# Routing 28 of 32 tiles of the last mixture of experts during the attention before it

## What is computed

```
x = x + tanh(g_xattn[1]) * _L1_xattn_ref(_layernorm(x), ctx_768, ...)   # 16 heads of 8, 1601 keys
x = x + tanh(g_ffn[1])   * _L1_ffn_ref(_layernorm(x), ...)              # below

gate_scores = x @ Wg + bg                      # 8 experts
top1   = argmax(gate_scores, axis=-1)
h = relu(einsum('btd,edh->beth', x, W1) + b1)  # 128 -> 512, of the chosen expert
y = einsum('beth,ehd->betd', h, W2) + b2       # 512 -> 128
out = einsum('betd,bte->btd', y, onehot(top1))
```

## Time and profile before

| | |
|---|---|
| median of 3 runs | 2914.64 us (2913.44 to 2914.93) |
| profiled execution: own time | 2913.21 us |
| profiled execution: span | 2911.2 us |
| its mean granted TensorE clock | 0.901 |
| PE / DVE / ACT / POOL busy | 83% / 75% / 72% / 43% of the span |

### The profile page before, as it was taken

One profiled execution on the slowest core, in us unless ns is written; L12 is line 12 of the kernel. 1 busy time (PEld: TensorE's weight loads), 2 busy tenths in 40 slices (PEclk: granted clock), 3 DMA queues, 4 the chain that ended last, 5 costly groups with the idle time before them and its releaser, 6 DMA issues. The chain is left out here.

```text
span 2911.2 us, 60895 instructions
## 1 busy us (share of the span) xinstructions
PE 2405.5 (83%) x19797; PEld 1252.2 (43%) x19797; DVE 2192.4 (75%) x8041; ACT 2106.3 (72%) x3547; POOL 1248.6 (43%) x1593
## 2 busy tenths in 40 slices
PE   7958888888888888667788479999999999999638
PEld 5735555555555555534522123333333333333337
DVE  8739878888888878636645799999999999993313
ACT  5749889898988888714412058888999888889325
POOL 1428777777777777713200412222322222200154
PEclk9979889988998899788888579999999999999669
DMA  8820000000000000081341113344443433330222
GB/s 245 266 79 12 13 14 15 14 13 14 13 18 19 14 15 14 5 290 55 51 117 35 68 49 104 89 98 108 106 104 95 105 89 97 95 68 2 59 93 68
DMA packets 163460, 205.76 MB, mean 71 GB/s; under 512 B 78588, under 2 KB 131106, under 8 KB 163126
## 3 DMA queue, kind: packets, MB, share of 16 engines
q1 hardware_dynamic: 152774, 161.80, 21.6%
q0 software_dynamic: 10352, 39.92, 4.0%
HBM read 135.19 MB, written 66.60 MB: 69 GB/s over the span
## 5 line engine op out<-in xcount | busy, mean ns | idle before, releaser
L2148 ACT ACTIVATE pb<-sps 128x512 f32<-128x512 f32 (+1 forms) x1664 | 896.1, 597 | 187.9 <-PE sps L2090 174.0
L2173 DVE TENSOR_REDUCE mx<-wps 128x2 f32<-128x1024 f32 x768 | 885.4, 1217 | 41.3 <-PE wps L2063 32.3
L1076 DVE MAX8 cand<-sc 128x8 f32<-128x46 f32 (+1 forms) x4480 | 602.7, 199 | 136.8 <-issue 77.9
L2105 PE MATMUL ops<-pb,va 128*9 128x256 f32 x6656 | 515.5, 382 | 8.2 <-issue 2.8
L852 PE MATMUL scores<-ctxT,qT 97*128 97x512 f32 (+1 forms) x1024 | 437.2, 576 | 80.5 <-ACT sc L964 69.5
L852 PEld LDWEIGHTS scores<-ctxT,qT 97*128 97x128 f32 x1024 | 206.6, 212 | 318.4 <-issue 218.6
L1943 POOL COPY va<-XX 128x128 f32<-128x128 f32 (+1 forms) x208 | 49.9, 292 | 626.0 <-PE ops L2105 618.4
L735 POOL TENSOR_TENSOR prf<-sc,prf 128x1601 f32<-128x1601 f32 x64 | 229.7, 3589 | 127.0 <-ACT prf L971 127.0
L827 PE MATMUL misc<-diag,prs 128*128 128x128 f32 (+1 forms) x1664 | 237.9, 300 | 7.0 <-issue 5.9
L735 POOL TENSOR_TENSOR prs<-sc,prs 128x1601 f32<-128x1601 f32 x64 | 230.6, 3604 | 16.8 <-ACT prs L971 13.8
L827 PEld LDWEIGHTS misc<-diag,prs 128*128 128x128 f32 (+1 forms) x1664 | 217.1, 207 | 17.3 <-issue 13.9
(11 more groups left out here) (407 smaller groups left out, 3953.5 us busy)
## 6 DMA issues: line engine op xcount, KB each, us to landing
FO<-keys SPq DMA_DIRECT2D x392, 50.0 KB
XX<-keys SPq DMA_DIRECT2D x392, 50.0 KB
ctxn<-in_ctx_dram SPq DMA_DIRECT2D x32, 576.0 KB
keys<-kpb POOLq DMA_DIRECT2D x42, 400.2 KB, 3.8
toep<-kernpad SPq DMA_DIRECT2D x8, 2048.0 KB, 14.9
values<-s_vs SPq DMA_DIRECT2D x16, 832.0 KB, 5.9
XX<-values SPq DMA_DIRECT2D x16, 832.0 KB, 4.8
keysf<-s_kf SPq DMA_DIRECT2D x16, 800.5 KB, 3.7
```

What stands on the lines that cost most here:

```text
L1076: st.add(v.max(cand[s % 2][:, 8 + n:8 + n + 7 * NP + 1:NP], sc[s % 4][:, c:c + w]))
L2105: ins = t.matmul(ops[VW * i:VW * i + DH1 + 1, 0:S], va[par][0:kn(kt), kt, 4 * g + i, :], pb[(UNITS * g + 2 * kt + i % 2) % 8][0:kn(kt), i ...
L2148: nc.scalar.activation(pb[(UNITS * g + u) % 8][0:rows_, :, :], sps[(UNITS * g + u) % SB][0:rows_, :, :], ACT.Exp).then_inc(p_ready, 1)
L2173: v.tensor_reduce(mx4[:, m // 2, :, 2 * g + m % 2, c], both, AX.X, ALU.max).then_inc(work_read, 1)
```

## The change

The work between attention and slots is taken apart by tiles. `TE` = 28 tiles belong to sequences that are finished when the last batch of attention begins its second group; `LT` = 4 tiles are those of the last two sequences.

- X's rows become 132 wide (`XR`): channels, mean, power of the variance, and the token's number twice. What is scattered to the sorted list is this raw row; a slot is normalised after it is loaded back, by a new DVE step `rows_of(s)`, into one of three tiles `xn`, and PE transposes `xn`.
- In `walk`, during the last batch: `prepare` (DVE: statistics of 28 tiles, POOL: the power, DVE: the first 8 normalised tiles) after step 8 of the first group; seven jobs `turn_rows` and seven jobs `logits` from step 2 of the second group on, two steps apart, and `places` at step 10 of the third group. POOL then scatters 28 tiles, still in the attention's block.
- The sorted list is filled in two parts. An expert's *whole* multiples of 128 among the first 28 tiles fill the first slots: at least `SURE` = 28 - 7 = 21 are full, whatever the data. What is left of each expert follows in 8 partial slots, and what the last 4 tiles add beyond those in further slots: 40 slots in all, one more than before.
- The last 4 tiles are normalised, routed and scattered between the first slots (`late_sums` to `late_who` on DVE, `late_turn`, `late_logits`, `late_sort` on PE, four scatters on POOL before that of slot 10). Slot 21 and later wait for them.
- The mixture's weights are loaded, and its constants and the split of its second bias made, at the start of the second attention, by SP and POOL, ahead of the second load of values on SP's queue.

The core of the diff:

```diff
-SLOTS = T + E - 1
-ROW = 2 * D + 4
+SLOTS = T + E
+ROW = D + 4
+TE = T - 2 * QT
+SURE = TE - E + 1
...
+                        if not follow and g == 0 and kt == 8:
+                            do.prepare()
+                        n = KT * (g - 1) + kt - 2
+                        if not follow and 0 <= n < 2 * (NE + 1):
+                            if n % 2 == 0 and n // 2 < NE:
+                                job(do.turn_rows, b, par, n // 2)
+                            if n % 2 == 1 and n > 1:
+                                job(do.logits, b, par, n // 2 - 1)
+                        if not follow and n == 2 * (NE + 1) + 5:
+                            job(do.places, b, par)
...
+            pool.wait_ge(pos_ready, 1)
+            for j in range(TE):
+                g_.indirect_dma_start(out=k.sorted[:, :], out_offset=bass.IndirectOffsetOnAxis(posi[:, j:j + 1], 0),
+                                      in_=k.XR[:, j, :], in_offset=None).then_inc(k.sorted_in, 16)
...
+            def turn_rows(gi, job, buf):
+                pe.wait_ge(hn_ready, gi + 1)
+                work(job)
+                for j in range(GT):
+                    ins = t.transpose(buf[:, j * P:j * P + P], hn[gi % 2][:, j, :], ident[:, :])
+                ins.then_inc(work_ready, 1)
...
+            def rows_of(s):
+                dve.wait_ge(x_in[s % XB], nth(s, XB))
+                if s >= 3:
+                    dve.wait_ge(xt_ready, s - 2)
+                x = xs[s % XB]
+                v.tensor_scalar(xn[s % 3][:, :], x[:, 0:D], x[:, D:D + 1], x[:, D + 1:D + 2], ALU.subtract, ALU.mult
+                                ).then_inc(xn_ready, 1)
...
+            slab(0)
+            slab(1)
+            late_sums()
+            rows_of(0)
+            rows_of(1)
+            late_rows()
+            late = {2: late_turned, 4: late_choice, 6: late_counts, 7: late_places, 9: late_who}
             for s in range(SLOTS):
                 if s + 2 < SLOTS:
                     slab(s + 2)
+                    rows_of(s + 2)
                 finish(s)
+                if s in late:
+                    late[s]()
...
             def turn_in(s):
-                pe.wait_ge(x_in[s % XB], nth(s, XB))
+                pe.wait_ge(xn_ready, s + 1)
                 if s >= 2:
                     pe.wait_ge(xT_ready, s - 1)
-                t.transpose(tp[s % 2][:, 0:P], xs[s % XB][:, 0:D], ident[:, :]).then_inc(xt_ready, 1)
+                t.transpose(tp[s % 2][:, 0:P], xn[s % 3][:, :], ident[:, :]).then_inc(xt_ready, 1)
```

More of the change, by code:

```diff
@@ L1806, in attention1_phase @@
         aoT = sb("aoT", [P, S])
+        hn = [sb(f"d_hn{i}", [P, GT, D]) for i in range(2)]
+        hT = [sb(f"d_hT{i}", [P, GT * P]) for i in range(2)]
+        stats, mv, var = sb("d_stats", [P, TE, 6]), sb("d_mv", [P, TE, 2]), sb("d_var", [P, TE])
+        lg, tmp, mx = sb("d_lg", [P, TE, E]), sb("d_tmp", [P, TE, E]), sb("d_mx", [P, TE])
+        ohb = sb("d_ohb", [P, TE, E], BF16)
+        cum = [sb(f"d_cum{i}", [P, TE, E], BF16) for i in range(2)]
+        steps, more = sb("d_steps", [P, TE]), sb("d_more", [P, E, TE])
+        whole, base_, ends = sb("d_whole", [P, E]), sb("d_base", [P, E]), sb("d_ends", [P, E])
+        upto, shift = sb("d_upto", [P, E, E]), sb("d_shift", [P, E])
+        past = sb("d_past", [P, SLOTS, E])
+        pos, posi, ids = sb("d_pos", [P, TE]), sb("d_posi", [P, TE], U32), sb("d_ids", [P, T], I32)
+        b2 = tmp[0:E, :, :].rearrange("p j e -> p (j e)")[:, 0:D]
+        parts = lg[0:E, :, :].rearrange("p j e -> p (j e)").bitcast(BF16)
+        b2h = [parts[:, n * D:n * D + D] for n in range(3)]
         wps = [ctx.enter_context(nc.psum_tensor(f"wps{i}", [P, 1024], F32)) for i in range(2)]
@@ L1831, in __init__ @@
                 self.group_end = self.result = self.turn = self.output = self.batch_end = Part.nothing
+                self.prepare = self.turn_rows = self.logits = self.places = Part.nothing
         START = HG * MJ + 2 + MJ
@@ L2254, in mixture1_phase @@
[L2254 to L2263, removed]
@@ L2264, in mixture1_phase @@
-        before, all1 = sb("e_before", [P, P], BF16), sb("e_all1", [P, P], BF16)
-        steps, slots = sb("e_steps", [P, T]), sb("e_slots", [P, SLOTS])
+        stats, mv, var = sb("e_stats", [P, LT, 6]), sb("e_mv", [P, LT, 2]), sb("e_var", [P, LT])
+        hn, hT = sb("e_hn", [P, LT, D]), sb("e_hT", [P, LT * P])
+        lg, tmp, mx = sb("e_lg", [P, LT, E]), sb("e_tmp", [P, LT, E]), sb("e_mx", [P, LT])
+        ohb = sb("e_ohb", [P, LT, E], BF16)
+        cum = [sb(f"e_cum{i}", [P, LT, E], BF16) for i in range(2)]
@@ L2266, in mixture1_phase @@
+        steps, more = sb("e_steps", [P, KMAX]), sb("e_more", [P, E, KMAX])
+        tot, extra, ends, base = sb("e_tot", [P, E]), sb("e_extra", [P, E]), sb("e_ends", [P, E]), sb("e_base", [P, E])
         upto = sb("e_upto", [P, E, E])
-        more = sb("e_more", [P, E, T])
-        tiles, ends, base = sb("e_tiles", [P, E]), sb("e_ends", [P, E]), sb("e_base", [P, E])
-        tri = sb("e_tri", [P, E, E])
         past = sb("e_past", [P, SLOTS, E])
-        who = sb("e_who", [P, SLOTS])
+        far, near, gone, who = (sb("e_" + n, [P, SLOTS]) for n in ("far", "near", "gone", "who"))
@@ L2342, in _ @@
[L2342 to L2350, removed]
@@ L2427, in _ @@
-            st.link(v.tensor_tensor(past[:, :, :], over(slots[:, :], E), rows(ends[:, :], SLOTS), ALU.is_ge))
-            st.link(v.tensor_reduce(who[:, :], past[:, :, :], AX.X, ALU.add))
-            st.link(v.tensor_scalar(whoi[:, :], who[:, :], float(E - 1), None, ALU.min))
-            dve.sem_inc(who_ready, 1)
             def slab(s):
```

437 lines of the change are left out of this document (281 added, 156 removed).

## The result

The changed kernel takes 3038.18 us, the median of 4 runs (3029.89 to 3041.08); the kernel before, on the same chip, 2914.78 (4 runs, 2913.44 to 2920.88). The ratio is 1.0427, 95% interval 1.0407 to 1.0446: slower by 4.3%. The forecast was 3020 us, 2950 to 3050, slower with 0.92: the direction, the mechanism and the range held, and the point is 18 us too low. The profiled execution took 3037.99 us; its span is 3036.1 where before's was 2911.2.

The account below looks back on a forecast made before the run. Bound by two serial stretches: POOL's 32 scatters, then slots with PE always busy. First transposition 48.9 us earlier, slots and late work 247 instead of 91.95 (+155): execution 2913.2 becomes 3019, median 3020 us; range 2950 to 3050.

Parts of the forecast that it names:

- When the early scatters begin: Last attention batch: work there shifts 16.3 us later, yet POOL's 28 early scatters end at 2757.8, 50.1 us earlier than before.
- Rival D: Last attention batch: PE stays at the lower clock after its 6.2 us wait; 25 us later, 3045 us; chance 0.10.
- E: Ahead of the slots: early scatters are not early, slots begin where they did; 3069 us; chance 0.03.
- At no cost: Loads before the last attention: weights delay second values some 13 us; nearly 50 us of DVE maxima cover it.
- About 5.0: Last early scatter to first transposition: about 5.0 us instead of 3.7, for DVE's two slabs, sums and first rows.
- The slot: Mixture slots: PE waits for DVE's chain; 4.5 us at full clock, 6.2 at the lower, 5.8 taken, instead of 2.2.
- the 12 us: First slots: late work of the last four tiles, 39 small DVE operations and some 2.5 us on PE; 6 to 18.
- the sum: All slots: 40 x 5.8 = 232, late work 12, drain 3, together 247 us instead of 91.95.
- three quarters of the slots at the lower clock: Mixture slots: three quarters taken at 6.2 us, one quarter at 4.5, giving 5.8 us a slot.
- B: Mixture slots: same wait on DVE's chain but the clock stays high; 40 x 4.5 = 180, 2968 us; chance 0.24.
- C: Mixture slots: DVE is ahead, rows are ready before PE asks, a slot stays at 2.2 us; 2866 us; chance 0.06.

## Why the prediction was right, and where it was off

*When the early scatters begin.* The working held step by step, from wherever X's update stands: from its end to `turn_rows` 14.4 us (13.9 foretold), PE's wait 6.62 (6.2 to 6.9), from `turn_rows` to `places` 32.0 (31.1; DVE's first operation on the places is at 2725.01, the hand-over taken as 0.85 as before), from there to the first scatter 7.1 (7.8), the 28 scatters 35.6 (35.6). The attention ends inside the scatters. Rival D did not occur, the granted clock being 1.00 from 2700 to 2725, and neither did E.

*"At no cost": wrong, by 7.8 us.* I had the delay about right (13 us; POOL was 11 late), but asked only who waits for the delayed work by a semaphore: DVE's need of the bias, 50 us away. Nobody waited for the splitting of the keys either; it cost because it ran at the same time as three small operations of DVE. The step that failed is the claim that 50 us of maxima cover the shift.

*"About 5.0" from the last scatter to the first transposition: wrong, 11.9.* The drain of POOL at the block's end, 7.53 us, was missing. The earlier trace rows could not price it: DVE began 0.43 us after the attention's end there, but POOL had issued no DMA for a long time when that block ended. The program's own end had a stretch of that length in plain sight, though, 7.6 us from the last output's scatter (2903.62) to the end of the span (2911.2). What that one is made of no run shows, beyond its shrinking to 5.3 where the drain stands at the attention's end.

*The slot: right, a little short.* 4.68 us at full clock (4.5 foretold), 6.36 where a whole slot ran at half, as from 2984.26 to 2990.62 in PE's timeline (6.2), 5.95 on the mean (5.8). Between the 40 transpositions stand 38 slots, since the first two follow each other at once: 38 x 0.15 = 5.7 us. The late work, with the filling of the first slots, cost more than the 12 us, inside its bounds of 6 to 18: the 12 slots to 2865.81 took 87.1 us, 12 x 5.95 are 71.4, so 15.7. The last two slots and the drain behind the last transposition took 10.4, where 2 x 5.8 + 3 = 14.6 stood in the sum. Together 252 instead of 247. That the mean came so close is partly luck: three quarters of the slots at the lower clock was taken without a row behind it, and 5.95 between 4.68 and 6.36 makes it 76%.

The errors add up: 8.3 (7.8 of it the split) + 7.6 (6.9 for the block's end, the rest smaller steps) + 5, less the 2.3 of the shorter tail, make the 19 us by which the execution is above its forecast.

*The rivals.* B, the chain with a high clock (2968 us), fell: the clock was 0.66, and the products in PE's gaps raised it to 1.00 and took 41 us off. The row of the earlier phase, 1.61 us idle and then half speed, was the better guide than the Trainium skill's page "TensorE: Matmul & The Clock Gate", section "Why this matters for your kernels", which names idle gaps longer than these as what brings the clock down. The trace differs: with gaps of 1.64 and 0.27 us in a slot of 5.95 the mean granted clock was 0.66, with 0.70 and 0.41 in a slot of 3.62 it was 1.00. C, that DVE is ahead, failed for the reason given, the place of `finish(s - 1)` in DVE's list; with one instruction moved past it, it came true, at 2.37 us a slot where C had 2.2.

## What to carry to other kernels

When an engine's list hands work to another engine and waits for the answer in the same turn of a loop, put the next turn's operand ahead of this turn's finish: here 0.34 us of work in the wrong place cost 139 us, more than a third of it through the clock. Work that is moved "under cover" has to be checked against what runs at the same time on other engines, here DVE's small operations beside POOL's long ones, and not only against who waits for it. And a block's end behind POOL's own DMAs has a price of its own: here leaving out the drain saved 8.1 us, of which 2.5 came back at the program's end.

## What was not expected of the hardware

- DVE's casts and subtractions of 128x32 took 1.5 to 3.7 us instead of 0.18 to 0.19 beside POOL's operations on 128x1601, each ending within 0.05 us of one of these.
- POOL's drain behind 28 indirect DMAs took 7.5 us, though they land much sooner: without the drain, the first rows had been loaded back, and their normalising began, 3.4 us after the end of the last scatter (2759.22 to 2762.57). Without it, the end of the program became 2.5 us longer.
- Seven useless products in nearly every slot made a program of 3038 us 41 us shorter, by keeping the granted clock of the later slots at 1.00.
